# A mixture-of-experts block after cross-attention: where the list of expert tiles is worked out, and how the last layer norm gets its statistics

## The reference, cut to what matters

```python
x = x + tanh(g_xattn[0]) * attention(layernorm(x), ctx, side)       # Q = q Wq.T + bq; K, V from ctx; scores Q K.T / 16 + weighted side
h = layernorm(x)
out = expert(h, shared)                                             # silu(h Wg.T) * (h Wu.T) @ Wd.T, inner width 512
probs = sigmoid(h @ Wr.T + rb); scores, idx = top_k(probs, 2)       # 8 routed experts, two for each row
out = out + sum(score_e * expert(h, e) for the two chosen)
x = x + tanh(g_ffn[0]) * out
f = layernorm(x)
rho[b, f, t] = sum_d w[d] * tanh((ctx @ Ws)[t, d] + (f @ W)[f, d] + bias[d])   # every row with every context row
att = softmax(rho, over t, masked); txt = att @ ctx
x = x + tanh(g_xattn[1]) * (tanh(txt @ Wcw + bcw) * f + tanh(txt @ Wcb + bcb))
q = clip(round(layernorm(x) / step), -127, 127) * step
x = x + tanh(g_ffn[1]) * (q @ (ternary - 1).T + bias)
```

## Time and profile before

| | |
|---|---|
| median of 3 runs | 1095.37 us (1093.33 to 1097.17) |
| profiled execution | 1098.02 us |
| its span, first to last instruction | 1096.3 us |
| mean granted clock of TensorE | 0.963 |
| busy PE, DVE, ACT, POOL | 996.7, 748.8, 668.2, 216.5 us |
| DMA | 164 MB, mean 150 GB/s |

### The profile page before, as it was taken

How to read it: one execution, slowest core, us unless ns; L and a number is a source line. 1 busy time by engine, 2 the same in 40 slices (tenths; PEclk the granted TensorE clock), 3 DMA queues, 4 the chain that set the end, 5 groups by cost and what they waited for, 6 DMA issues and landing times.

```text
span 1096.3 us, 23452 instructions
## 1 busy us (share of the span) xinstructions
PE 996.7 (91%) x8772; PEld 771.5 (70%) x8772; DVE 748.8 (68%) x2110; ACT 668.2 (61%) x966; POOL 216.5 (20%) x257
## 2 busy tenths in 40 slices
PE   6889999999999999999999999999999999966661
PEld 2568777787779999977777777777777777622220
DVE  2566788877653345644578678578588488898876
ACT  1211111111101111399999999999999999999990
POOL 1032123331250003121122121131131121310000
PEclk9859999999999999999999999999999999999895
DMA  8011101100039999876466456656665564100000
GB/s 254 25 63 58 39 30 63 44 34 15 30 104 333 336 332 341 305 246 214 160 222 229 176 197 228 202 198 204 207 217 197 186 231 155 40 16 21 1 20 19
DMA packets 114053, 164.21 MB, mean 150 GB/s; under 512 B 13235, under 2 KB 70068, under 8 KB 113940
## 3 DMA queue, kind: packets, MB, share of 16 engines
q1 hardware_dynamic: 104004, 135.57, 36.9%
q0 software_dynamic: 9936, 27.15, 6.7%
HBM read 138.69 MB, written 23.99 MB: 148 GB/s over the span
## 4 chain that ended last, share of the span: by engine, by line
PE 72%; DVE 11%; issue 7%; ACT 7%; DMA 2%; POOL 1%; SPq 0%; POOLq 0%; DVEq 0%; ACTq 0%
PE bank L1130 21%; PE bank L1313 16%; PE bank L1292 11%; PE bank L1135 6%; PE bank L1283 3%; PE bank L1172 2%; PE bank L1116 2%; PE bank L1300 2%; ACT arena L656 2%; PE bank L1187 2%; PE bank L1219 1%; PE bank L1245 1%; DMA picked<-expert_rows,found_at 1%; DVE ln_moe_stats L748 1%; DVE x L818 1%
## 5 line engine op out<-in xcount | busy, mean ns | idle before, releaser
L1130 PEld LDWEIGHTS bank<-rowsT,expert_w 128*128 128x128 f32 x2272 | 270.8, 192 | 10.3 <-issue 6.2
L1130 PE MATMUL bank<-rowsT,expert_w 128*128 128x128 f32 x2272 | 276.6, 275 | 0.5 <-DVE rowsT L938 0.5
L648 ACT ACTIVATE act<-bank 128x512 f32<-128x512 f32 x103 | 61.3, 595 | 211.9 <-PE bank L1130 115.2
L1292 PE MATMUL bank<-expert_w,act 128*128 128x256 f32 x568 | 138.6, 387 | 1.8 <-DVE rowsT L938 1.7
L573 POOL DMA_DIRECT2D expert_rows<-rows_out x71 | 42.6, 601 | 492.7 <-DVE rows_out L955 492.7
L1135 PE MATMUL bank<-normT,shared_w 128*128 128x256 f32 x512 | 126.8, 396 | 0.0
L955 DVE COPY rows_out<-bank 128x256 f32<-128x256 f32 x71 | 30.1, 425 | 141.2 <-PE bank L1292 140.5
L664 ACT ACTIVATE tanhs<-shared_w,txtT 128x512 f32<-128x512 f32 x168 | 122.0, 726 | 2.1 <-DVE shared_w L981 2.1
L1292 PEld LDWEIGHTS bank<-expert_w,act 128*128 128x128 f32 x568 | 102.2, 190 | 28.8 <-issue 15.9
L665 ACT ACTIVATE tanhs<-shared_w,txtT 128x512 f32<-128x512 f32 x168 | 122.0, 726 | 0.0
L1135 PEld LDWEIGHTS bank<-normT,shared_w 128*128 128x128 f32 x512 | 98.3, 198 | 17.3 <-issue 3.0
(11 more groups left out here) (230 smaller groups left out, 1483.8 us busy)
## 6 DMA issues: line engine op xcount, KB each, us to landing
expert_w<-in_WgT SPq DMA_DIRECT2D x71, 512.0 KB, 4.0
expert_w<-in_WuT SPq DMA_DIRECT2D x71, 512.0 KB, 5.2
expert_w<-in_WdT SPq DMA_DIRECT2D x71, 512.0 KB, 6.7
rows_in<-rows_by_expert SPq DMA_DIRECT2D x71, 128.0 KB, 5.8
expert_rows<-rows_out POOLq DMA_DIRECT2D x71, 128.0 KB, 4.3
x<-in_x SPq DMA_DIRECT2D x8, 512.0 KB, 4.2
out<-x SPq DMA_DIRECT2D x16, 256.0 KB, 2.7
score<-in_fside SPq DMA_DIRECT2D x8, 128.0 KB, 2.3
```

The costliest lines, as they stand in the source:

```text
L648: e.activation(act[n % 2][:, :], banks[2 * (n % 2)][:, :], ACT.Tanh, scale=0.5).then_inc(s_tanh, 1)
L1130: got = e.matmul(bank[:, i * P:(i + 1) * P], w[:, at:at + P], t[:, c * P:(c + 1) * P], start=c == 0, stop=c == DC - 1)
L1292: got = e.matmul(row_bank[:, 0:D], act[n % 2][:, c * P:(c + 1) * P], w[:, at:at + D], start=c == 0, stop=c == IC - 1)
```

## The change

- The step "opened" is done twice in all, once for the first 28 row tiles and once for the last four, in the last image's routing; it works from running totals of each expert at each row tile (the count product now gives them for every row tile) instead of from each row, and each partition finds the one tile whose place in the list is its own number. The low part and tile number of each slot move into "find".
- The count product and its matrices are bf16, and it has up to 72 columns instead of 40.
- The query's bias comes from a table on all partitions, made in the prologue, and is added on VectorE where the side input is scaled.
- The last norm takes its mean and variance from the mixing norm (x is only stretched and shifted in between), so it needs no statistics; "apply" comes after the quantization, and the two weighted sums are one.
- PLACES, PAIRS and LAGS have other numbers.

The diff, cut: of replaced functions only the new lines are shown, and indentation is reduced.

```diff
-PLACES = {"attend": 72, "route": 36, "late": -59, "gather_first": -71, "norm_first": -27.5, "gather": 8.5, "norm": 44,
-          "mix_in_end": -3, "feature": 20, "sum": 5, "preadd": 3, "mix_out": 8, "mix_out_end": 50.5}
-PAIRS = {0: 2, 1: 4, 2: 4, 3: 4, 4: 4, 5: 4, 6: 8, 7: 12}
+PLACES = {"opened": 25.5, "attend": 72, "route": 36.5, "late": -59, "gather_first": -68, "norm_first": -28, "gather": -1, "norm": 42.5,
+          "mix_in_end": -3, "feature": 20, "sum": 5, "preadd": 3, "mix_out": 9, "mix_out_end": 50}
+PAIRS = {0: 7, 1: 4, 2: 4, 3: 7, 4: 4, 5: 4, 6: 10, 7: 13}
 LAGS = {
-    "sync": {"fetch": -3, "load_side": -1.5, "narrow": -5},
-    "gpsimd": {("power", "lin"): -1, ("power", "moe"): -1},
-    "scalar": {"gate_act": -2.5, "soft_rho": 1, "softmax": -2, "spread": 7.5, "squash": 0.5, "tanh": 1.5, ("turn", "att"): -0.5,
-               ("turn", "mix"): -0.5, "turn_e": 1.5},
-    "vector": {"add": 0.5, "add_bias": 1.5, ("aggr", "att"): 2.5, ("aggr", "lin"): 1, "choice": -1.5, "convert": -20.5, "find": 4.5,
-               "gate_act": 3, "linear": 5, "narrow": 2, ("newton", "att"): 2, ("newton", "lin"): 2, ("newton", "mix"): 1,
-               ("newton", "moe"): 1, "place": -0.5, ("power", "att"): 3, "preadd": -1.5, "quantize": 1, "rho": -2.5, "rsum": 1,
-               ("scale", "mix"): 0.5, ("scale", "moe"): -0.5, "side": -3.5, "soft_rho": -0.5, "softmax": 0.5, ("stats", "att"): 2.5,
-               ("stats", "mix"): 1.5, "step": 2, "sums": 3.5, "text": 10.5, ("turn", "moe"): -0.5, "turn_q": -2, "turn_rows": 1.5,
-               "weigh": -1},
-    "tensor": {"count": -1.5, "feature": -2, "linear": 2.5, "scores": -0.5, "spread": 2.5, "sum": 0.5, "text": 8,
-               ("turn", "mix"): -0.5, "weigh": -2},
+    "sync": {"fetch": 4, "load_side": -5.5, "narrow": 0.5},
+    "gpsimd": {("power", "lin"): -2, "scatter": -0.5},
+    "scalar": {"gate_act": -1, "soft_rho": 1, "softmax": -2, "spread": 5, "squash": 1, "tanh": 1.5, ("turn", "att"): -0.5,
+               ("turn", "mix"): -2.5, "turn_e": -3.5},
+    "vector": {"add": 0.5, "add_bias": 6, "affine": 0.5, ("aggr", "att"): 1, ("aggr", "lin"): -0.5, ("aggr", "mix"): 1,
+               ("aggr", "moe"): -0.5, "apply": 1.5, "choice": -1, "convert": -24.5, "feature": -2, "find": 3, "gate_act": 3,
+               "linear": 4, "narrow": 2, ("newton", "lin"): -1.5, ("newton", "mix"): -0.5, ("newton", "moe"): 1, "opened": 1.5,
+               "place": -0.5, ("power", "att"): -0.5, "preadd": -3, "quantize": -3, "rho": -3.5, "rsum": -0.5, "side": -3.5,
+               "sigmoid": 1.5, "soft_rho": -0.5, "softmax": 0.5, ("stats", "att"): 2.5, ("stats", "mix"): 1, "step": -3, "sums": 3.5,
+               "text": 10.5, "tiles": -1, ("turn", "moe"): -0.5, "turn_q": 1.5, "turn_rho": 0.5, "turn_rows": 0.5, "weigh": -1,
+               "weigh_ws": -0.5},
+    "tensor": {"count": -1.5, "feature": -1.5, "logits": -0.5, "scores": -0.5, "spread": 5.5, "sum": 0.5, "text": 8,
+               ("turn", "mix"): -0.5, "turn_rho": -3.5, "up": 2.5, "weigh": 1},
...
-        steps[-self.ST] += [("opened", b)]
         if b == self.B - 1:
+            steps[-self.ST] += [("opened", 1)]
...
-        return ([[("rho", b)], [], [("turn_rho", b)], [("soft_rho", b)], [("rsum", b)], [("weigh_ws", b)], [("weigh_bs", b)],
-     [("squash", b)], [("affine", b)], [("apply", b)]] + self.norm("lin", b, False)
-    + [[("step", b)], [("quantize", b, 0)], [("quantize", b, 1)], [("add_bias", b)], [], [("turn_q", b)],
-       [("linear", b, 0)], [("linear", b, 1)]])
+        return [[("rho", b)], [], [("turn_rho", b)], [("soft_rho", b)], [("rsum", b)], [("weigh_c", b)], [("squash", b)], [("stretch", b)],
+    [("power", "lin", b)], [("affine", b)], [("newton", "lin", b)], [("step", b)], [("quantize", b, 0)], [("quantize", b, 1)],
+    [("apply", b)], [("turn_q", b)], [("add_bias", b)], [("linear", b, 0)], [("linear", b, 1)]]
...
+            if b == B - 1:
+    place([[("opened", 0)]], at - PLACES["opened"], at - PLACES["opened"])
...
+        n = ST * b
         bank, done = product(("count", b))
+        counts = bank[:, 0:(2 * ST + 1) * E].rearrange("p (i e) -> p i e", e=E)
+        carry = totals[:, n:n + 1, :].to_broadcast([P, ST, E])
+        if b == 0:
+            e.wait_ge(s_consts, CONSTS)
+        e.wait_ge(s_chain, links[0])
+        link(e.tensor_tensor(posn[:, :, :], counts[:, 0:ST, :], carry, ALU.add))
+        e.tensor_tensor(totals[:, n + 1:n + ST + 1, :], counts[:, ST + 1:, :], carry, ALU.add).then_inc(done, 1)
         for j in range(2):
+            chain(lambda: e.tensor_tensor(rt[:, :, :], hot[j][:, :, :], posn[:, :, :], ALU.mult))
+            chain(lambda: e.tensor_reduce(slots[:, n:n + ST, j], rt[:, :, :], AX, ALU.add))
+            got = linked(lambda: e.tensor_copy(slot_of[j][:, n:n + ST], slots[:, n:n + ST, j]))
...
     elif name == "opened":
+        g, = k
+        first, last = (0, OPEN) if g == 0 else (OPEN, NT)
+        n = last - first
+        b = (last - 1) // ST
+        per = [P, n, E]
+        new = tiles_by[:, first + g:last + 1, :]
+        t0, t1 = tiles_by[:, first:last, :], tiles_by[:, first + 1:last + 1, :]
+        ping, pong = sums[0][:, 0:n, :], sums[1][:, 0:n, :]
+        more, base = opening[:, 0:n, :], before_step[:, 0:n]
+        e.wait_ge(s_misc[misc["count", b][0]], misc["count", b][1])
+        chain(lambda: e.tensor_scalar(new, totals[:, first + g:last + 1, :], 1.0 / P, 0.5 - 0.5 / P, ALU.mult, ALU.add))
+        chain(lambda: e.tensor_scalar(new, new, ROUND, None, ALU.add))
+        chain(lambda: e.tensor_scalar(new, new, -ROUND, None, ALU.add))
+        chain(lambda: e.tensor_reduce(base, t0, AX, ALU.add))
+        link(e.tensor_tensor(more, t1, t0, ALU.subtract))
+        link(e.tensor_tensor(ping[:, :, 4:], t1, t0, ALU.subtract))
+        chain(lambda: e.tensor_tensor(pong[:, :, 4:], ping[:, :, 4:], ping[:, :, 3:3 + E], ALU.add))
+        chain(lambda: e.tensor_tensor(ping[:, :, 4:], pong[:, :, 4:], pong[:, :, 2:2 + E], ALU.add))
+        chain(lambda: e.tensor_tensor(pong[:, :, 4:], ping[:, :, 4:], ping[:, :, 0:E], ALU.add))
+        chain(lambda: e.tensor_tensor(pong[:, :, 4:], pong[:, :, 4:], base.unsqueeze(2).to_broadcast(per), ALU.add))
+        chain(lambda: e.tensor_tensor(more, pong[:, :, 4:], more, ALU.subtract))
+        link(e.tensor_scalar(pong[:, :, 4:], pong[:, :, 4:], lane_from[:, 0:1], None, ALU.is_gt))
+        chain(lambda: e.scalar_tensor_tensor(out=pong[:, :, 4:], in0=more, scalar=lane_from[:, 0:1], in1=pong[:, :, 4:],
+                                             op0=ALU.is_le, op1=ALU.mult))
+        link(e.tensor_tensor(ping[:, :, 4:], t0, more, ALU.subtract))
+        chain(lambda: e.scalar_tensor_tensor(out=more, in0=ping[:, :, 4:], scalar=lane_code[:, 0:1], in1=pong[:, :, 4:],
                                              op0=ALU.add, op1=ALU.mult))
+        chain(lambda: e.tensor_reduce(opened[:, g:g + 1], more.rearrange("p n e -> p (n e)"), AX, ALU.add))
+        if g == 1:
+            chain(lambda: e.tensor_tensor(opened[:, 0:1], opened[:, 0:1], opened[:, 1:2], ALU.add))
+            linked(lambda: e.tensor_scalar(listed[:, :], ident[:, 0:RT], opened[:, 0:1], None, ALU.mult)).then_inc(s_opened, 1)
...
+        chain(lambda: e.tensor_scalar(code, slot, 1.0 / P, 0.5 / P - 0.5, ALU.mult, ALU.add))
+        chain(lambda: e.tensor_scalar(code, code, ROUND, None, ALU.add))
+        chain(lambda: e.tensor_scalar(code, code, -ROUND, None, ALU.add))
+        chain(lambda: e.scalar_tensor_tensor(out=low, in0=code, scalar=-float(P), in1=slot, op0=ALU.mult, op1=ALU.add))
...
+    elif name == "weigh_c":
+        b, = k
+        products = out_work[:, 0:2 * ST * T].rearrange("p (k i t) -> p k i t", k=2, t=T)
+        per = [P, 2, ST, T]
+        if b:
+            e.wait_ge(s_misc_mm, misc["linear", b - 1, 1][2])
+        chain(lambda: e.tensor_tensor(products, rho_e[:, :, :].unsqueeze(1).to_broadcast(per),
+                                      ctx_w[:, :, b * T:(b + 1) * T].unsqueeze(2).to_broadcast(per), ALU.mult))
+        chain(lambda: e.tensor_reduce(weighed[:, :, :], products, AX, ALU.add))
+        linked(lambda: e.tensor_tensor(weighed[:, :, :], weighed[:, :, :],
+                                       sm["rsum"][:, :].unsqueeze(1).to_broadcast([P, 2, ST]), ALU.mult)).then_inc(s_ws, 1)
+        link(e.tensor_scalar(sm["gr"][:, :], ln_of("mix", b)["r"][:, :], GX1, None, ALU.mult))
+    elif name == "stretch":
+        b, = k
+        var, w1, t = ln_of("mix", b)["mv"][:, :, 1], sm["w1"][:, :], sm["t"][:, :]
+        e.wait_ge(s_squash, b + 1)
+        chain(lambda: e.tensor_tensor(w1, weighed[:, 0, :], sm["gr"][:, :], ALU.mult))
+        chain(lambda: e.scalar_tensor_tensor(out=t, in0=w1, scalar=1.0, in1=var, op0=ALU.add, op1=ALU.mult))
+        chain(lambda: e.scalar_tensor_tensor(out=t, in0=w1, scalar=1.0, in1=t, op0=ALU.add, op1=ALU.mult))
     elif name == "affine":
         b, = k
```

(23 more changed lines are left out.)

163 lines of the change are left out of this document (55 added, 108 removed).

## The result

The changed kernel took a median of 1065.32 us (1063.58 to 1072.46, 4 runs) beside 1094.35 us (1092.38 to 1097.17, 4 runs) for the kernel before on the same chip: a ratio of 0.9745 with a 95% interval of 0.9695 to 0.9795. A second comparison on another chip, with 6 and 11 runs, gave 1065.9 beside 1097.25: 0.9722 (0.9700 to 0.9745). The forecast was 1061.4 in a range of 1047 to 1081: right in direction and size, 4 us too fast. The profiled execution has a span of 1063.6 us (time 1065.3, forecast 1064.0), 32.7 less than the profiled one of before.

The account below looks back on a forecast made before the run. TensorE bounds the kernel to 938 us (nearly full before 334), then ScalarE, then a closing VectorE chain. 11 + 13 + 1.5 + 0 + 4.5 + 4 = 34 us off 1098.0 gives 1064.0 profiled, median 1061.4; 8-in-10 range 1047 to 1081.

Parts of the forecast that it names:

- Part 1: TensorE work removed before 334 us: query bias off TensorE (5.0 us), count product in bf16 (5.2); 11 us, 5 to 13.
- Part 2: TensorE gaps before 334 us, mostly from the "opened" block delaying VectorE's residual add: 70% of 18.5 us, 13 saved.
- rival B: Before 334 us: fewer TensorE gaps also give clock back, 6 to 8 us more; 1048 to 1053, chance 14%.
- an image still over 33 us: Sign that would prove part 2 wrong; a steady image was forecast at 30 to 32 us instead of 34.3.
- the nearest row: Basis for the bf16 count: eight bf16 products of 128 columns in 0.61 us, so 0.38 for five, against 1.03.
- Rival A: Before 334 us: only the work goes, gaps keep the same sum; 21 us gained, or 1074; chance 18%.
- Part 3: Hand-over at 334 us: earlier route brings the last count 1.8 us forward, 1.5 taken (0 to 2); tile list covered.
- partly done before the last count: Hand-over: the list's two runs of small VectorE operations, 4 and 6 us, counted as covered with 12 us to spare.
- Part 4: Routed tiles, 334 to 938 us: same products, moved places; cost 0 (-2 to +4).
- Rival C: Routed stage: VectorE becomes the bound and sends products late, 39 us against 34 gained; 1100, chance 6%.
- Part 5: ScalarE after 938 us: six more wide-tanh pairs (3.9 us) and a later gate activation (1.2); 4.5 taken, 0 to 5.1.
- Rival E: Tail: VectorE's adds are late and ScalarE waits, so nothing gained there; 9 us less gain, 1070, chance 9%.
- Part 6: Closing chain for the last image: merged operations save 0.5 us, norm without statistics 3.86, apply 0.3 late; 4 us saved.

## Why the prediction was right

**The sum.** Forecast 11 + 13 + 1.5 + 0 + 4.5 + 4 = 34, measured in the profiled executions 25.0 before the routed stage, 0 in it, 3.6 in the tail, 4.0 in the closing chain: 32.6. The forecast for the first three was 25.5. This sum is right by two errors that cancel, and they can be told apart by image:

- An image at full clock went from about 34.3 to 30.07 us, 4.2 less. Parts 1 and 2 gave 3.0 (0.62 + 0.65 + 70% of 2.45). Undone one by one, the bias is worth 0.83 an image, the count 0.95, and the block an estimated 2.4 (the run with it back): together the 4.2. No steady image keeps a gap that VectorE ended; one of 0.78, behind ScalarE, is left.
- Against that, six images lost 8.4 us to half clock, where those of before lost none. No term of the sum had this, in either sign; rival B alone spoke of the clock. The sign "an image still over 33 us" did come, with 33.4 us in the third row above, but by the clock and not by VectorE as part 2 meant it.
- The stretch from the last logits to the first routed product is 44.8 us before and 44.6 and 42.9 in the two profiles of the changed kernel. That the three terms met the 25.0 to half a microsecond is partly this profile: by the second one it is 28.3.

**Part 1.** Mechanism right, both terms too small. In the run with the bias back its row takes the forecast 0.62 us, and besides it the shared product in front takes 1.83 us from start to start instead of 1.72 and the scores behind 1.84 instead of 1.74. The step that failed is the nearest row for the count: eight bf16 products of 128 columns gave 0.38, the rows show 0.14. The Trainium skill, page "TensorE: Matmul & The Clock Gate", section "Wait — 56ns, not 53.3ns?", by which the prediction had estimated 0.13 to 0.16, was the better guide; the trace agrees with it here.

**Part 2.** Right in cause: the kernel with the block back shows the two gaps again, behind the block, and loses 18 to 21 us, of which a part is half clock behind the gaps. The 0.78 before the weighed sums went as said; a like one came before the logits, where the new order puts turned rows and logits together. The prediction did not look for it. Rival A (the gaps stay) is out.

**Part 3.** The step that failed: "partly done before the last count" was taken for covered. Only the list's second half had 12 us of cover; the first half was in front of the last choice on an engine that runs in order, and TensorE waited 3.30 us for the count (1.62 in the second profile, where part of the same time passed at half clock). So the 1.8 us from an earlier count did not come: it starts 9.15 us after the last logits in both profiles, 9.09 before. With the block out of its way it came after 7.4, so the 1.8 themselves were right. Three other places for the block were tried, and each moved the wait: to the list's own product, to a shared activation product, to the last image's turned exponentials.

**Part 4.** 0 forecast, 0.0 measured (0.3 in the second profile). Rival C did not come in the changed kernel, but the run with the old tables shows its mechanism at 2.4 us a wait and 20 us in the stage: the new tables are what prevents it.

**Part 5.** 3.6 of 4.5. The six pairs bring 3.1 (or 2.5) and not 3.9, and ScalarE waits 1.92 us at 927.96 for VectorE. Rival E was near: four pairs more already lose 5.6.

**Part 6.** 4.0 of 4; from the weighed sums' scaling to the norm 3.01 us (1047.11 to 1050.12) against 6.81, where 2.95 was forecast.

**Rival B** (whose own terms, 6 to 8 and the 5.5 left in part 2, give 1048 to 1050 and not up to 1053) had the place right (clock in these stages, several us) and the condition wrong. It said that fewer gaps give clock back. The changed kernel has fewer gaps than before and more time at half clock, 20.5 us (17.0 in the second profile) against 6.8 between 90 us and the hand-over. The prediction also read that the clock held 1.00 from 85 us on; in the trace of before it did so until 291.9. The 40 to 85 us window stayed at a mean of 0.70 in both.

## What to carry to other kernels

Work out a stage image by image at one level of the clock, and list the granted clock beside each: a right sum can hide a gain of 7 and a loss of 8. Ask of every block moved to "somewhere with slack" which instruction stands right behind it on that engine, since on an in-order engine the slack of its result is not the slack of what it holds up. When code is taken out, the written order must be fitted again, and best by stage: here the code alone brought 14 us of 29, and one more change of order at the logits brought another 8.5.
